# Spreading the cross-attention queries over the head masks on ScalarE instead of by small transfers

## The chip, the cores and the metric

One core of a Trainium2 chip runs the whole kernel. The metric is device time in microseconds (us), the median of repeated runs. The core has five engines that run side by side, each through its own instruction queue in program order: TensorE (matmuls, PE in the rows), VectorE (DVE), ScalarE (ACT), GpSimd (POOL) and SyncE (SP), which here only issues transfers. They are ordered against each other by semaphores that the kernel waits on by hand. Data is moved by 16 DMA engines.

## The reference, cut to what matters

A decoder layer on x of 32 x 128 x 128 with a context of the same shape: top-32 self-attention, then 16-head cross-attention, then a routed feed-forward layer with 8 experts. The change is in the cross-attention, whose heads have only 8 of the 128 features each:

```python
Q = (query @ Wq.T + bq).reshape(B, S, H, HD).transpose(0, 2, 1, 3)   # H = 16, HD = 8
K = (key @ Wk.T + bk).reshape(B, S, H, HD).transpose(0, 2, 1, 3)
V = (value @ Wv.T + bv).reshape(B, S, H, HD).transpose(0, 2, 1, 3)
scores = jnp.einsum('bhqd,bhkd->bhqk', Q, K) / jnp.sqrt(jnp.asarray(HD, Q.dtype))
weights = jax.nn.softmax(scores, axis=-1)
out = jnp.einsum('bhqk,bhkd->bhqd', weights, V)
```

## The kernel before, in words

The 32 batches are worked in 8 groups of 4 (g = 0 to 7). Cross-attention of group g is **pass** g. A pass has 8 **steps** (n = 0 to 7), two for each batch j. In the same pass the queues also carry the self-attention and the projections of groups g+2 and g+3 and the normalisation, routing and storing of group g-1. After pass 7 come 39 tiles of the feed-forward layer. The order of every queue is written out by hand in `run(g)` and `step(n, before, after)` of each engine; there is no scheduler.

Scores of 16 heads are made on TensorE in four **strips** of 32 partitions, each with four heads of 8 features. One strip's matmul has 32 x 128 weights and a moving operand of 32 x 512: the 128 tokens four times, once for each head of the strip, with all features of the other three heads zero. This "masked" copy is what the change is about. There are two such products. `s1` (L1565) takes natural queries and masked keys, and VectorE takes from its result the maximum per head and query (`head_max`, L1004, `neg_hmax`). `s2` (L1576) takes natural keys and masked queries. Into the same bank `s2_shift` (L1583) adds minus the maximum, and ScalarE's `exps` (L1309, `weights`) take the exponential. `pv` (L1607) multiplies by the values. The maxima reach `s2_shift` by `hmax_split` on VectorE (L1017, L1019), a transpose on TensorE (`hmax_rows`, L1593) and `hmax_out` on ScalarE (L1300, `hmax_t`).

Waits that matter below: `s2` waits until the exponentials of two strips before are done, as it overwrites their bank; `s1` waits for VectorE's maxima in the same way; the first two strips of a `pv` wait for `hmax_t` of the next batch. So each step has s2 x2, s1 x2, (hmax_rows), s2_shift x2 on TensorE, and (hmax_out), exps x2 on ScalarE.

The natural queries of group e = g+2 are projected at the end of pass g (step 7) and ScalarE copies them with their bias to `q_nat`, a part of the buffer `q_room` (`cross_queries`, L1302, semaphore `xq_ready`). The masked queries, `q_masked`, lie in `q_room` too, in a ring of two groups (`Q_RING`), each four blocks of 128 x 512. For group 0 ScalarE makes the four blocks itself, by a copy with a factor per partition, `head_mask`, that is one or zero (L1503). For groups 1 to 7 SyncE issues 16 transfers per group, 8 partitions x 2 KB each, that put the features of one head in their place in blocks that GpSimd had set to zero at the start (L919) or that have stayed zero since (L599, `mask_queries`, in pass g for group g+1). The keys are spread in the same way by 16 transfers per group, and this stays. `s2` of a group's first strip waits for all of `xq_masked`.

In the rows ScalarE's `xn<-x` is `normed_x1` (L1316 x4, step 5, group g+2), `xn_t`, scores and other self-attention buffers are pieces of `self_room`, and `ctx_t` also takes the transposed `xn2`.

Of the kernel before, what the change touches and what calls it, by code (L numbers as in the profile page):

```python
# [6 lines left out]
def preln_decoder_kernel(nc, T, out):  # L7
# [6 lines left out]
    ACT = mybir.ActivationFunctionType  # L14
# [5 lines left out]
    H, HD = 16, 8  # L20
    G = 4
# [24 lines left out]
    with ExitStack() as stack:  # L46
# [111 lines left out]
        def carve(which, n):  # L158
# [36 lines left out]
            attn_done x1_ready x1_bv_ready  # L195
            xn2_transposed xn2_t_ready xq_done xq_ready xq_masked first_masked mask_made early_step taken_step
            ctx_transposed ctx_t_ready xk_done xk_ready xk_masked xv_done xv_ready ones_made
            s1_done s1_max hmax_step hmax_split hmax_transposed hmax_t_ready s2_done s2_exp pv_done pvt_ready att_transposed
            wsum_inv_ready attended_ready x2_ready
            feats_transposed feats_t_ready aff_done aff_ready aff_max_ready aff_exp_ready aff_den_ready alpha_ready  # L200
            rstd2_step rstd2_ready base_ready pay_ready tokens_ready blank_made blanks_stored bv_made zeros_made q_zeros_made k_zeros_made wvo_done wvo_ready
            w1_loaded w1_rest_loaded b1_done b1_ready iota_made
# [77 lines left out]
        def later(g, first):  # L280

            return not isinstance(g, int) or g >= first
# [278 lines left out]
        def _(sp):  # L561
# [38 lines left out]

            def mask_queries(g):

                if not 1 <= g < NG:
                    return
                wait_alone(sp, s["xq_ready"], g + 1)
                if g == 1:
                    wait_alone(sp, s["q_zeros_made"], 1)
                if later(g, 2):
                    wait_alone(sp, s["xq_masked"], 16 * H * (g - 1))
                if later(g, Q_RING):  # L610
                    wait_alone(sp, s["s2_done"], 16 * (g - Q_RING + 1))
                spread_heads(q_masked, q_nat[:, (g % 3) * GS:(g % 3 + 1) * GS], (g % Q_RING) * MASKED, "xq_masked")

            def mask_keys(g):
# [14 lines left out]
            def run(g):  # L629
                if g >= 0:  # L630
                    load_later_x(g)
                    mask_queries(g + 1)
                if 0 < g + 3 < NG:
                    wait_alone(sp, s["ctx_transposed"], g + 3)
                    wait_alone(sp, s["ctx_loaded"], 16 * (g + 3))
                    load_ctx(g + 3)
                mask_keys(g + 2)
                if g < 0:
                    load_later_x(g)
                    mask_queries(g + 1)  # L640
                if isinstance(g, int) and g == NG - 3:
                    load_biases()
# [118 lines left out]
        def _(pool):  # L761
# [156 lines left out]

            pool.memset(q_masked[:, MASKED:2 * MASKED], 0.0).then_inc(s["q_zeros_made"], 1)  # L919
            norm_rstd(pool, 0, 0)  # L920
# [365 lines left out]
        def _(act):  # L1286
# [101 lines left out]
            def cross_queries(e):  # L1388
                if 0 <= e < NG:
                    if later(e, 3):  # L1390
                        act.wait_ge(s["s2_done"], 16 * (e - 2))
                    evacuate(q_nat[:, (e % 3) * GS:(e % 3 + 1) * GS], cross_bank[:, :], "xq_done", e + 1, "xq_ready", 2)

            def normed_x1(e):
                if 0 <= e < NG:
                    if later(e, 1):
                        act.wait_ge(s["xn2_transposed"], e)
                    norm(1, e, x1[:, :], xn2[:, :])
# [19 lines left out]
            def run(g):  # L1418
                has_f, has_c, has_e, has_s = stages(g)
                e, h = g + 2, g + 3  # L1420

                def step(n, before, after):

                    scores_first = isinstance(g, int) and g == 0 and n == 0
                    g1, j1 = following(g, n // 2, 1)
                    if not scores_first:
                        before()
                    if n % 2 == 1 and has_c and g1 < NG:
                        hmax_out(g1, j1)
                    if has_c:  # L1430
                        exps(g, n // 2, n % 2 * 2)
                        exps(g, n // 2, n % 2 * 2 + 1)
                    if scores_first:
                        before()
                    after()
                    batches = G * g + n // 2
                    if n % 2 == 0 and has_c and batches > 0:
                        evacuate(pvt[:, :], pvt_bank[:, 0:256], "pv_done", 4 * batches, "pvt_ready")
                    if g == NG - 1 and n == 7:
                        evacuate(pvt[:, :], pvt_bank[:, 0:256], "pv_done", 4 * B, "pvt_ready")  # L1440
# [59 lines left out]
            act.wait_ge(s["mask_made"], 2)  # L1500
            act.wait_ge(s["xq_ready"], 1)
            for m in range(G):
                act.activation(at(q_masked, m * GS, GS), q_nat[:, 0:GS], ACT.Copy, scale=head_mask[:, m:m + 1])\  # L1503
                   .then_inc(s["first_masked"], 1)
            probs_out(1)
# [7 lines left out]
        def _(pe):  # L1513
# [54 lines left out]
            def s2(g, j, u):  # L1568
                q = 16 * g + 4 * j + u
                if later(g, 1) or q >= 2:  # L1570
                    pe.wait_ge(s["s2_exp"], q - 1)
                if j == 0 and u == 0 and g == 0:
                    pe.wait_ge(s["first_masked"], G)
                if j == 0 and u == 0 and g > 0:
                    pe.wait_ge(s["xq_masked"], 16 * H * g)
                pe.matmul(s2_bank[:, (u % 2) * GS:(u % 2 + 1) * GS], natural(k_nat, g, j, u), masked(q_masked, Q_RING, g, j, u),  # L1576
# [334 lines left out]
```

## Time and profile before

| | |
|---|---|
| median of 3 runs | 411.51 us (410.72 to 412.42) |
| the profiled execution | 409.8 us, its span 408.1 us |
| span around the profile | 1.7 us |
| TensorE / VectorE / ScalarE / GpSimd busy | 87% / 73% / 59% / 48% of the span |
| pass 0 begins (first `s2`) | about 50 us |
| passes 1 to 4, each | about 31.3 us |
| mean granted TensorE clock | 0.949 of full |

A timeline row gives start and duration in us, the engine, the line of the kernel, the operation, the output and inputs, and how many instructions are merged (x2 counts two; an fp32 matmul shows as two). Behind it in brackets stands how long the engine was idle just before it and what ended that. Durations overlap: an engine takes up the next instruction before the record of the last one ends, so starts are the better ruler.

### The profile page before, as it was taken

What the parts mean: (1) busy time and instruction counts of PE and PEld (TensorE: products, weight loads), DVE (VectorE), ACT (ScalarE), POOL (GpSimd) and SP (SyncE); (2) the same over time, 40 slices, a digit from 0 to 9 for tenths busy, and PEclk for the clock granted to TensorE, in tenths of its full rate; (3) what the DMA queues carried; (4) which work ended last, traced back from release to release, by engine and by line L of the source; (5) the groups of instructions that cost most, each with busy time, mean ns of one, the idle gap of its engine ahead of it and who ended that gap; (6) DMA issues with size and microseconds to landing.
All of it is one profiled execution on the core that took longest, in us unless ns stands there. A gap on an engine that the chain in (4) does not pass through costs nothing.

```text
span 408.1 us, 11367 instructions
## 1 busy us (share of the span) xinstructions
PE 353.6 (87%) x3499; PEld 248.9 (61%) x3499; DVE 296.8 (73%) x1218; ACT 240.8 (59%) x527; POOL 195.7 (48%) x348
## 2 busy tenths in 40 slices
PE   5988989998999999999998899998696857899990
PEld 4766645545555655654654555555486747899980
DVE  6799846997898898897798858577653646566660
ACT  1464446666777777776766665656263445677750
POOL 4687400320650573574483375736576245344451
PEclk9799969999999999999999999999769698999996
DMA  5415201232121122221211122000322133433310
GB/s 136 155 23 174 55 13 25 51 103 49 31 77 29 46 84 54 51 82 51 51 45 36 24 88 52 24 35 28 86 74 83 50 125 120 112 92 92 87 50 0
DMA packets 30155, 26.96 MB, mean 66 GB/s; under 512 B 5891, under 2 KB 25479, under 8 KB 30096
## 3 DMA queue, kind: packets, MB, share of 16 engines
q1 hardware_dynamic: 26016, 19.59, 18.3%
q0 software_dynamic: 2784, 6.37, 4.6%
q8 instruction: 29, 0.48, 0.5%
q10 hardware_dynamic: 1296, 0.28, 0.5%
q14 instruction: 30, 0.25, 0.2%
HBM read 14.73 MB, written 8.01 MB: 56 GB/s over the span
## 4 chain that ended last, share of the span: by engine, by line
PE 50%; DVE 12%; issue 11%; ACT 9%; SPq 3%; POOL 2%; DVEq 2%; another core or an unknown queue 1%; DMA 1%; ACTq 0%; POOLq 0%
PE s_bank L1576 13%; PE pvt_bank L1607 5%; PE s_bank L1583 4%; PE s_bank L430 4%; DVE q_room L466 3%; PE cross_bank L1518 3%; ACT weights L1309 3%; PE cross_bank L1523 2%; ACT self_room L1300 2%; PE s_bank L1565 2%; ACT xn L1316 2%; PE cross_bank L1671 2%; PE cross_bank L1644 2%; PE att_bank L1729 2%; DVE x_in L481 2%
## 5 line engine op out<-in xcount | busy, mean ns | idle before, releaser
L1004 DVE TENSOR_REDUCE neg_hmax<-s_bank 128x4 f32<-128x512 f32 x128 | 82.4, 687 | 40.6 <-PE s_bank L1565 40.2
L1309 ACT ACTIVATE weights<-s_bank 128x512 f32<-128x512 f32 x128 | 69.8, 596 | 29.1 <-PE s_bank L1583 25.1
L1576 PE MATMUL s_bank<-q_room,k_room 32*128 32x512 f32 x256 | 78.9, 639 | 0.2
L1565 PE MATMUL s_bank<-k_room,q_room 32*128 32x512 f32 x256 | 76.9, 647 | 0.2 <-DVE neg_hmax L1004 0.2
L519 POOL DMA_INDIRECT out<-x_in,k_room x39 | 37.9, 972 | 48.1 <-DVE x_in L481 33.4
L805 POOL TENSOR_TENSOR x<-x_bv,attended 128x128 f32<-128x128 f32 x32 | 14.5, 453 | 76.4 <-DVE attended L1031 76.4
L466 DVE TENSOR_TENSOR q_room<-s_bank,b_cols 128x512 f32<-128x512 f32 x39 | 27.0, 692 | 30.4 <-PE s_bank L430 21.8
L1607 PE MATMUL pvt_bank<-weights,xv 128*32 128x128 f32 x1024 | 42.3, 283 | 3.3 <-ACT hmax_t L1300 3.1
L430 PE MATMUL s_bank<-k_room,self_room 128*128 128x128 f32 x312 | 44.7, 290 | 0.0
L501 ACT ACTIVATE self_room<-w,gamma_t 128x512 f32 x39 | 28.2, 722 | 23.5 <-PE s_bank L430 15.8
L430 PEld LDWEIGHTS s_bank<-k_room,self_room 128*128 128x128 f32 x312 | 41.3, 206 | 0.0
L816 POOL DMA_INDIRECT routed_rows<-pay,slot x32 | 33.0, 1030 | 12.1 <-issue 7.6
L1607 PEld LDWEIGHTS pvt_bank<-weights,xv 128*32 128x32 f32 x1024 | 25.1, 111 | 18.9 <-ACT weights L1309 9.1
L1576 PEld LDWEIGHTS s_bank<-q_room,k_room 32*128 32x128 f32 x256 | 24.9, 183 | 15.6 <-issue 8.2
L996 DVE MATCH_REPLACE8 self_room<-best,self_room 128x128 f32<-128x128 f32 x128 | 34.1, 284 | 0.0
L1583 PEld LDWEIGHTS s_bank<-hmax_t,head_sel 32*128 32x128 bf16 x512 | 20.3, 93 | 17.6 <-issue 14.4
L507 ACT ACTIVATE q_room<-q_room 128x512 f32<-128x512 f32 x39 | 24.6, 630 | 10.4 <-DVE q_room L466 5.3
L727 POOL TENSOR_SCALAR var_eps<-moments 128x4 f32<-128x4 f32 x24 | 4.9, 203 | 53.3 <-DVE moments L688 52.8
L1583 PE MATMUL s_bank<-hmax_t,head_sel 32*128 32x128 bf16 x512 | 29.9, 217 | 0.0
L444 PE MATMUL pvt_bank<-w,q_room 128*128 x160 | 23.7, 294 | 6.2 <-ACT q_room L507 6.2
L1300 ACT ACTIVATE hmax_t<-pvt_bank 128x128 bf16<-128x128 bf16 x32 | 8.9, 277 | 32.8 <-PE pvt_bank L1593 31.1
L990 DVE MAX8 best<-self_room 128x8 f32<-128x128 f32 x128 | 27.7, 282 | 0.0
(213 smaller groups left out, 739.0 us busy)
## 6 DMA issues: line engine op xcount, KB each, us to landing
k_room<-routed_rows SPq DMA_DIRECT2D x39, 130.0 KB
w<-in_w SPq DMA_DIRECT2D x16, 256.0 KB, 4.0
x_in<-in_x SPq DMA_DIRECT2D x8, 256.0 KB, 3.3
ctx_in<-in_ctx SPq DMA_DIRECT2D x8, 256.0 KB, 2.9
k_room<-k_room SPq DMA_DIRECT2D x128, 16.0 KB
q_room<-q_room SPq DMA_DIRECT2D x112, 16.0 KB
routed_rows<-blank SPq DMA_DIRECT2D x9, 130.0 KB
out<-x_in,k_room POOLq DMA_INDIRECT x39
```

The lines of the kernel that those rows point to most:

```text
L430: m = pe.matmul(s1_bank[:, (k % 2) * F + c * 128:(k % 2) * F + (c + 1) * 128], ffn_w1[k % 2][:, c * 128:(c + 1) * 128], ffn_row_t[k % 2], ...
L466: dve.tensor_tensor(by_chunk(ffn_hid[k % 2]), by_chunk(s1_bank[:, (k % 2) * F:(k % 2 + 1) * F]), spread(at(b1_cols, e * FC, FC).rearrange( ...
L501: act.activation(ffn_w1[k % 2], at(w1, e * F, F), ACT.Identity, scale=at(gamma_t, e, 1)).then_inc(s["w1_picked"], 1)
L519: pool.indirect_dma_start(out=out_rows, out_offset=bass.IndirectOffsetOnAxis(ap=ffn_row[k][:, TOKEN:TOKEN + 1].bitcast(U32), axis=0), in_= ...
L816: pool.indirect_dma_start(out=rows, out_offset=bass.IndirectOffsetOnAxis(ap=slot[:, at0:at0 + 1].bitcast(U32), axis=0), in_=pay[:, at0, :] ...
L996: dve.match_replace(at(left, b * S, S), best8[:, b, r, :], at(src, b * S, S), TAKEN)\
L1004: dve.tensor_reduce(neg_hmax[:, first:first + 4], bank.rearrange("p (h k) -> p h k", k=S), AX.X, ALU.max, negate=True).then_inc(s["s1_max" ...
L1309: act.activation(weights[:, u, :], s2_bank[:, (u % 2) * GS:(u % 2 + 1) * GS], ACT.Exp, scale=HEAD_SCALE).then_inc(s["s2_exp"], 1)
L1565: pe.matmul(s1_bank[:, (u % 2) * GS:(u % 2 + 1) * GS], natural(q_nat, g, j, strip(u)), masked(k_masked, K_RING, g, j, strip(u)), start=Tru ...
L1576: pe.matmul(s2_bank[:, (u % 2) * GS:(u % 2 + 1) * GS], natural(k_nat, g, j, u), masked(q_masked, Q_RING, g, j, u), start=True, stop=False)
L1583: m = pe.matmul(s2_bank[:, (u % 2) * GS + i * S:(u % 2) * GS + (i + 1) * S], head_sel[32 * u:32 * (u + 1), i, :], hmax_t[32 * u:32 * (u + ...
L1607: m = pe.matmul(pvt_bank[32 * i:32 * (i + 1), (u % 2) * S:(u % 2 + 1) * S], xv[:, block:block + 32], weights[:, u, i * S:(i + 1) * S], sta ...
```

## The change

`mask_queries` moves from SyncE to ScalarE. For groups 1 to 7 ScalarE makes the four masked blocks by the same operation as for group 0, one behind each of four steps of the pass before: steps 2, 4, 6 and 7 (in pass 0 steps 3, 4, 6 and 7). SyncE's 16 transfers per group and GpSimd's one setting to zero of 128 x 2048 go. `xq_masked` now counts four per group.

```diff
@@ SyncE @@
-            def mask_queries(g):
-
-                if not 1 <= g < NG:
-                    return
-                wait_alone(sp, s["xq_ready"], g + 1)
-                if g == 1:
-                    wait_alone(sp, s["q_zeros_made"], 1)
-                if later(g, 2):
-                    wait_alone(sp, s["xq_masked"], 16 * H * (g - 1))
-                if later(g, Q_RING):
-                    wait_alone(sp, s["s2_done"], 16 * (g - Q_RING + 1))
-                spread_heads(q_masked, q_nat[:, (g % 3) * GS:(g % 3 + 1) * GS], (g % Q_RING) * MASKED, "xq_masked")
@@ SyncE, run(g) @@
                 if g >= 0:
                     load_later_x(g)
-                    mask_queries(g + 1)
@@ GpSimd @@
-            pool.memset(q_masked[:, MASKED:2 * MASKED], 0.0).then_inc(s["q_zeros_made"], 1)
@@ ScalarE @@
+            def mask_queries(e, m):
+                if 0 <= e < NG:
+                    act.wait_ge(s["xq_ready"], e + 1)
+                    if later(e, Q_RING):
+                        act.wait_ge(s["s2_done"], 16 * (e - Q_RING + 1))
+                    at0 = (e % Q_RING) * MASKED + m * GS
+                    act.activation(at(q_masked, at0, GS), q_nat[:, (e % 3) * GS:(e % 3 + 1) * GS], ACT.Copy,
+                                   scale=head_mask[:, m:m + 1]).then_inc(s["xq_masked"], 1)
@@ ScalarE, run(g) @@
+                mask_steps = (3, 4, 6, 7) if g == 0 else (2, 4, 6, 7)
                     if n % 2 == 0 and has_c and batches > 0:
                         evacuate(pvt[:, :], pvt_bank[:, 0:256], "pv_done", 4 * batches, "pvt_ready")
+                    if n in mask_steps:
+                        mask_queries(g + 1, mask_steps.index(n))
@@ TensorE, s2 @@
-                if j == 0 and u == 0 and g == 0:
-                    pe.wait_ge(s["first_masked"], G)
-                if j == 0 and u == 0 and g > 0:
-                    pe.wait_ge(s["xq_masked"], 16 * H * g)
+                if j == 0 and u == 0:
+                    pe.wait_ge(s["xq_masked"], G * (g + 1))
```

How the queues stand at the places of which the prediction speaks. First ScalarE's queue in steps 4 and 5 of pass 1 (passes 0 to 5 have the same rows here, pass 0 without `feats_t`), before:

```order
L1309 ACTIVATE weights<-s_bank 128x512 x2
L1300 ACTIVATE feats_t<-cross_bank 128x512
L1300 ACTIVATE pvt<-pvt_bank 128x256
L1316 ACTIVATE xn<-x,mean_rstd,rstd 128x128 x4
L1300 ACTIVATE hmax_t<-pvt_bank 128x128
L1309 ACTIVATE weights<-s_bank 128x512 x2
```

and now (its lines stand 16 lower there):

```order
L1293 ACTIVATE weights<-s_bank 128x512 x2
L1284 ACTIVATE feats_t<-cross_bank 128x512
L1284 ACTIVATE pvt<-pvt_bank 128x256
L1384 ACTIVATE q_room<-q_room,head_mask 128x512
L1300 ACTIVATE xn<-x,mean_rstd,rstd 128x128 x4
L1284 ACTIVATE hmax_t<-pvt_bank 128x128
L1293 ACTIVATE weights<-s_bank 128x512 x2
```

One masking operation (L1384) has come between the copy of `pvt` and `normed_x1`, ahead of `hmax_out` and the exponentials of step 5.

Second ScalarE's queue from step 7 of pass 5 to step 1 of pass 6, where no group is left for `context`, before:

```order
L1309 ACTIVATE weights<-s_bank 128x512 x2
L1302 ACTIVATE q_room<-cross_bank,bias_cols 128x512
L1309 ACTIVATE weights<-s_bank 128x512 x2
L1300 ACTIVATE pvt<-pvt_bank 128x256
L1300 ACTIVATE hmax_t<-pvt_bank 128x128
```

and now:

```order
L1293 ACTIVATE weights<-s_bank 128x512 x2
L1286 ACTIVATE q_room<-cross_bank,bias_cols 128x512
L1384 ACTIVATE q_room<-q_room,head_mask 128x512
L1293 ACTIVATE weights<-s_bank 128x512 x2
L1284 ACTIVATE pvt<-pvt_bank 128x256
L1284 ACTIVATE hmax_t<-pvt_bank 128x128
```

The fourth masking operation of group 6 has come between the copy of group 7's natural queries and the first exponentials of pass 6. In passes 0 to 4 the same row is followed by `context`'s copy of `ctx_t`; at the end of pass 6 there is no copy of natural queries, and it stands right behind the exponentials.

Third SyncE's queue in passes 4 to 6, before:

```order
L599 DMA q_room<-q_room 8x512 x16
L567 DMA ctx_in<-in_ctx 128x4x128
L599 DMA k_room<-k_room 8x512 x16
L599 DMA q_room<-q_room 8x512 x16
L599 DMA k_room<-k_room 8x512 x16
L585 DMA x_in<-in_b 128x1024
L599 DMA q_room<-q_room 8x512 x16
```

and now:

```order
L567 DMA ctx_in<-in_ctx 128x4x128
L599 DMA k_room<-k_room 8x512 x32
L585 DMA x_in<-in_b 128x1024
```

The transfers of the queries are gone, and what stood behind them moves up.

## Rows read from the trace of the kernel before

**Rows 1.** the page's part 1: busy us (share) and instructions of each engine.

```profile
PE 353.6 (87%) x3499; PEld 248.9 (61%) x3499; DVE 296.8 (73%) x1218; ACT 240.8 (59%) x527; POOL 195.7 (48%) x348
```

**Rows 2.** pass 4: us; busy PE, PEld, DVE, ACT, POOL; PEclk; DMA share, GB/s.

```profile
183.30:215.10 31.80, 29.53 (x340) 17.77 (x339) 26.95 (x122) 21.31 (x49) 17.98 (x34) 1.00 0.18 48
```

**Rows 3.** the chain that ended last, in pass 4.

```profile
204.52 0.73 ACT xn L1316 x2
```

**Rows 4.** group 0's masking: ns min/median/max, first and last start; and its timeline.

```profile
L1503 ACT ACTIVATE q_room<-q_room,head_mask x4: 708/708/713, 41.6 to 43.5; 128x512 f32<-128x512 f32 x4
...
41.64 2.54 ACT L1503 ACTIVATE q_room<-q_room,head_mask 128x512 f32<-128x512 f32 x4
```

**Rows 5.** timeline of SyncE's queue, pass 1.

```profile
88.72 10.68 SPq L599 DMA_DIRECT2D q_room<-q_room  x16
```

**Rows 6.** ScalarE's exponentials in 89.4:99.4 and 112.5:119.3 (count, busy us, mean ns).

```profile
L1309 ACT ACTIVATE weights<-s_bank 128x512 f32<-128x512 f32 x4 | 2.2, 595 | 0.7 <-PE s_bank L1583 0.7
...
L1309 ACT ACTIVATE weights<-s_bank 128x512 f32<-128x512 f32 x5 | 2.8, 610 | 0.0
```

**Rows 7.** timeline of ScalarE, pass 4 and the start of pass 5.

```profile
197.96 0.28 ACT L1300 ACTIVATE hmax_t<-pvt_bank 128x128 bf16<-128x128 bf16 x1 [2.26 <-PE pvt_bank L1593]
...
204.38 1.65 ACT L1316 ACTIVATE xn<-x,mean_rstd,rstd 128x128 f32<-128x128 f32 x4
...
205.92 0.28 ACT L1300 ACTIVATE hmax_t<-pvt_bank 128x128 bf16<-128x128 bf16 x1
...
211.49 0.21 ACT L1409 ACTIVATE aff_exp<-aff_max 128x4 f32<-128x4 f32 x1 [0.52 <-DVE aff_max L1131]
...
212.15 0.28 ACT L1300 ACTIVATE hmax_t<-pvt_bank 128x128 bf16<-128x128 bf16 x1 [0.45 <-issue]
...
213.77 0.69 ACT L1302 ACTIVATE q_room<-cross_bank,bias_cols 128x512 f32<-128x512 f32 x1 [0.26 <-PE cross_bank L1523]
```

**Rows 8.** timeline of TensorE, pass 4 and the start of pass 5.

```profile
188.11 0.70 PE L1576 MATMUL s_bank<-q_room,k_room 32*128 32x512 f32 x2
...
189.19 0.23 PE L1593 MATMUL pvt_bank<-ident_bf,hmax_parts 128*128 128x128 bf16 x1
...
206.35 0.64 PE L1607 MATMUL pvt_bank<-weights,xv 128*32 128x128 f32 x16 [0.44 <-ACT hmax_t L1300]
...
210.46 0.70 PE L1576 MATMUL s_bank<-q_room,k_room 32*128 32x512 f32 x2
...
211.83 0.23 PE L1593 MATMUL pvt_bank<-ident_bf,hmax_parts 128*128 128x128 bf16 x1
...
215.11 0.70 PE L1576 MATMUL s_bank<-q_room,k_room 32*128 32x512 f32 x2
```

**Rows 9.** timeline of VectorE, pass 4.

```profile
202.48 1.29 DVE L1004 TENSOR_REDUCE neg_hmax<-s_bank 128x4 f32<-128x512 f32 x2 [1.17 <-PE s_bank L1565]
...
209.43 1.29 DVE L1004 TENSOR_REDUCE neg_hmax<-s_bank 128x4 f32<-128x512 f32 x2
```

**Rows 10.** timeline of TensorE, step 7 of pass 0.

```profile
83.83 1.26 PE L1576 MATMUL s_bank<-q_room,k_room 32*128 32x512 f32 x4
...
86.17 0.23 PE L1593 MATMUL pvt_bank<-ident_bf,hmax_parts 128*128 128x128 bf16 x1
```

**Rows 11.** ScalarE in passes 5 and 6.

```profile
234.54 1.65 ACT L1316 ACTIVATE xn<-x,mean_rstd,rstd 128x128 f32<-128x128 f32 x4 [0.77 <-POOL mean_rstd L743]
...
243.56 0.69 ACT L1302 ACTIVATE q_room<-cross_bank,bias_cols 128x512 f32<-128x512 f32 x1 [0.22 <-PE cross_bank L1523]
...
259.80 0.28 ACT L1300 ACTIVATE hmax_t<-pvt_bank 128x128 bf16<-128x128 bf16 x1 [0.88 <-PE pvt_bank L1593]
...
266.50 1.08 ACT L1309 ACTIVATE weights<-s_bank 128x512 f32<-128x512 f32 x2
```

**Rows 12.** TensorE: first `s2` of passes 6 and 7.

```profile
243.96 0.70 PE L1576 MATMUL s_bank<-q_room,k_room 32*128 32x512 f32 x2
...
267.32 1.00 PE L1576 MATMUL s_bank<-q_room,k_room 32*128 32x512 f32 x2
```

More of the change, by code:

```diff
@@ L195, in preln_decoder_kernel @@
             attn_done x1_ready x1_bv_ready
-            xn2_transposed xn2_t_ready xq_done xq_ready xq_masked first_masked mask_made early_step taken_step
+            xn2_transposed xn2_t_ready xq_done xq_ready xq_masked mask_made early_step taken_step
             ctx_transposed ctx_t_ready xk_done xk_ready xk_masked xv_done xv_ready ones_made
@@ L200, in preln_decoder_kernel @@
             feats_transposed feats_t_ready aff_done aff_ready aff_max_ready aff_exp_ready aff_den_ready alpha_ready
-            rstd2_step rstd2_ready base_ready pay_ready tokens_ready blank_made blanks_stored bv_made zeros_made q_zeros_made k_zeros_made wvo_done wvo_ready
+            rstd2_step rstd2_ready base_ready pay_ready tokens_ready blank_made blanks_stored bv_made zeros_made  k_zeros_made wvo_done wvo_ready
             w1_loaded w1_rest_loaded b1_done b1_ready iota_made
@@ L639, in run @@
                     load_later_x(g)
-                    mask_queries(g + 1)
                 if isinstance(g, int) and g == NG - 3:
@@ L1500, in _ @@
             act.wait_ge(s["mask_made"], 2)
-            act.wait_ge(s["xq_ready"], 1)
             for m in range(G):
-                act.activation(at(q_masked, m * GS, GS), q_nat[:, 0:GS], ACT.Copy, scale=head_mask[:, m:m + 1])\
-                   .then_inc(s["first_masked"], 1)
+                mask_queries(0, m)
             probs_out(1)
```

## The prediction

> **What bounds the kernel now.** I read the page's busy shares first: TensorE is busy for 87% of the span, VectorE 73%, ScalarE 59% [rows 1]. That says TensorE, but the shares are means over stages, so I took one pass. In pass 4 TensorE is busy for 29.53 of 31.80 us, VectorE for 26.95 and ScalarE for 21.31, with a granted clock of 1.00, the 2.4 GHz level [rows 2]. ScalarE thus has 10.5 us of room in a pass, and four operations more would fit as a sum. What counts is where they are put, since it works in order and TensorE waits for it at several places. The chain that ended last shows one: in each of passes 1 to 4 it leaves TensorE once for `normed_x1` (the row shown, four such) [rows 3]. ScalarE's timeline says why: `normed_x1` begins at 204.38 and `hmax_out` at 205.92, both without idle time before them [rows 7], and TensorE stands for 0.44 us until `pv` can start at 206.35, 0.15 after `hmax_out` ends at 206.20 [rows 8]. This is step 5, and ScalarE is the bound there. VectorE is the second clock: from 202.48 on it works without a gap through steps 5, 6 and 7 [rows 9].
>
> **What is removed, and what that is worth.** SyncE issues group 2's 16 transfers from 88.72 to 99.40 (10.68 us) [rows 5], while the `s2` that needs them comes with pass 2, about 31 us after 89. Nothing in the passes waits for them. The same holds for what SyncE has behind them: the context of group g+3 and the masked keys of group g+2 are used a pass later. GpSimd's setting to zero lies at the start, where it then waits for VectorE anyway. So I put the removed part at 0. The bounds: nothing below 0 from waits, since no wait goes; whether the traffic itself slows the engines is seen in ScalarE's exponentials, 595 ns each with these transfers in flight and 610 without [rows 6]. What keeps it at 0 is that all of it is covered by a whole pass of TensorE work.
>
> The Trainium skill bears on this from two sides (DMA: Bandwidth & Descriptors, Rules for kernel authors). It says that transfers under 64 KB are mostly overhead, and it also says that the fixed cost of a transfer is hidden when it is issued early and waited for late. These transfers are 16 KB, so the first would count 112 overheads as a gain, the second none; the sum by the second is the one above, and the trace agrees with it by the 10.68 us that end 20 us early [rows 5].
>
> **What one masking operation costs.** Group 0 has the very operation: 708 ns each, and four of them take 2.54 us, so one begins (2.54 - 0.71) / 3 = 0.61 us after the other [rows 4]. 28 of them are 17 us more on ScalarE. For each I ask what it stands in front of.
>
> *Step 2 (and step 3 in pass 0).* Before `hmax_out` ScalarE is idle for 2.26 us [rows 7]. Hidden: 0. Without this cover it would be 0.61 a pass.
>
> *Step 6.* `affinity_exp` waits 0.52 us for VectorE and the next `hmax_out` is idle for 0.45 more [rows 7], 0.97 together against 0.61. Hidden: 0. In pass 6 the least such gap at its steps 2, 4 and 6 is 0.88 us [rows 11]: 0.
>
> *Step 4, passes 1 to 4.* Here nothing is idle: `normed_x1` starts at once behind `pvt` [rows 7]. The operation moves `normed_x1`, `hmax_out` and the exponentials of step 5 by 0.61, and with them `pv` and the `s2` of step 6, where the matmuls wait in line. Behind it TensorE is in order, so the loss goes on until TensorE meets a wait on something that was not moved. There is one, in step 7: a step without such a wait has 1.08 us from `s2` to `hmax_rows` (188.11 to 189.19), step 7 has 1.37 (210.46 to 211.83) [rows 8]. The 0.29 more is the second `s1` waiting for VectorE's maxima, whose pair starts at 209.43 with no idle time before it [rows 9], and would still do so, since its `s1` results would come at about 209.0. So 0.29 is paid back: 0.61 - 0.29 = 0.32 a pass, 1.3 us for four. VectorE itself isn't late. The bounds: 0.61 if nothing is paid back, 0 if VectorE holds more.
>
> *Step 4, pass 0.* In step 7 of that pass the same distance is 86.17 - 83.83 = 2.34 us [rows 10], 1.26 more than 1.08, so a delay of 0.61 vanishes: 0.
>
> *Step 4, pass 5.* `normed_x1` is idle for 0.77 us waiting for GpSimd [rows 11], more than 0.61: 0.
>
> *Step 7, into passes 1 to 5.* The fourth block comes behind the copy of the new natural queries, which starts at 213.77 [rows 7]. The masking starts some 0.57 later (the pitch of that copy, estimated as its 0.69 less the usual overlap of 0.12), ends 0.71 after that, and TensorE needs 0.15 (as with `pv` above): 213.77 + 0.57 + 0.71 + 0.15 = 215.20, while `s2` of pass 5 now starts at 215.11 [rows 8]. So 0.09 late; passes 1 to 4 begin in the same way. Five times: 0.4 us. It is so small because TensorE first has `pv` and four transposes of the context. Bounds: 0 and 0.3 each, if a weight load waits too.
>
> *Step 7 of pass 5, into pass 6.* No group is left whose context would be transposed, so the cover is gone. The copy starts at 243.56 [rows 11], the block is ready for TensorE at 243.56 + 1.43 = 244.99, and `s2` now starts at 243.96 [rows 12]: **1.03 us late**. Queued behind it on TensorE are both `s1` and `s2_shift`, for which VectorE's maxima and ScalarE's exponentials wait; all move along.
>
> *Step 7 of pass 6, into pass 7.* There is no copy, and the block comes behind two exponentials that start at 266.50 and take 1.08 together [rows 11]. With the usual overlap it starts at 267.47, ends at 268.18, and `s2` can go at 268.33 instead of 267.32 [rows 12]: **1.01 us late**. Bounds of these two: 0.9 and 1.2 each.
>
> **Sum.** 1.3 + 0.4 + 1.0 + 1.0 = 3.7 us. The profiled execution took 409.8, so it would take 413.5. That execution is 1.7 under the median of the runs, 411.5, to which the same 3.7 is added: **415.2 us**, 0.9% slower. With all lower bounds the sum is 0 + 0 + 1.8 = 1.8, with all upper ones 5 x 0.61 + 5 x 0.3 + 2.4 = 7.0.
>
> **The rivals.**
> (a) *Nothing is paid back at step 7*, because VectorE's work moves with TensorE's: 5 x 0.61 + 0.4 + 2.0 = 5.5, so 417.0. For it: the maxima do read what TensorE writes. Against it: VectorE has no gap there.
> (b) *More is paid back*: VectorE is busy for 26.95 of 31.80 us [rows 2], and if its order holds the passes, the 0.32 and the 0.09 vanish and perhaps part of the steps into 6 and 7. That is 2.0 or less, 413.5 or less, no difference that can be told (a measurement of this kernel tells about 0.5%, 2 us, from no change). Against it: VectorE waits for TensorE in each pass (1.17 us in pass 4 [rows 9]).
> (c) *The transfers cost something now*, so that the kernel gets faster. They are in flight for 7 x 10.7 = 75 us. To end even they must slow what lies beside them by 3.7 / 75 = 5%, and for 2 us of gain by 8%; at 10% it would be 7.5 - 3.7, so 407.7. Against it: 595 ns with and 610 ns without them [rows 6], no sign of even 1% in this direction. The Trainium skill (SBUF — State Buffer, SBUF: two separate sides) says that engines and DMA use different ports and cannot contend, by which this rival gains 0; the trace agrees.
> (d) *More is lost*: gaps that just suffice (0.97 in step 6, 0.77 in pass 5) do not, at 0.3 us for five passes each, on top of (a): 419 or more.
>
> **Chances.** The forecast 0.60, (a) 0.15, (b) 0.15, (c) 0.05, (d) 0.05. Slower by over 0.5% are the forecast, (a) and (d): 0.80. Within 0.5%: 0.15. Faster: 0.05. The range leaves out (c), (d) and the lower half of (b): 412.9 to 418.2.
>
> **What would show it.** In the profile after: about 28 masking operations more of 0.71 us on ScalarE and 112 transfers fewer. In passes 1 to 4 the idle time of TensorE before `pv` in step 5 grows from 0.44 to about 1.05, and `s2` to `hmax_rows` in step 7 shrinks from 1.37 to 1.08; each of these passes is 0.4 longer. The first `s2` of passes 6 and 7 stands behind ScalarE's masking, each by 1 us. Pass 0 is unchanged. I would be wrong if `pv` waits no longer in step 5, if the first `s2` of pass 6 is held by something else, or if the feed-forward tiles, which the change doesn't touch, take a different time.

## The result, and the profile of the changed kernel

| | before | changed |
|---|---|---|
| median of 4 runs each | 411.12 us (408.89 to 412.42) | 416.98 us (415.88 to 422.52) |
| ratio, 95% interval | | 1.0155 (1.0099 to 1.0212) |
| profiled execution | 409.8 us, span 408.1 | 415.88 us, span 414.1 |
| mean granted TensorE clock | 0.949 | 0.938 |

The ratio says about 1.5% slower; the medians differ by 5.9 us, where 3.7 us had been forecast. Each ratio here and below leaves out the runs more than 1.5% above the fastest of their kernel, and since a fall of TensorE's clock makes just such a run, the experiments give the mean of all runs beside it.

The page of the kernel before, the queue of the hardware transfers (packets, MB, share), and the groups of `s2` (L1576) and `pv` (L1607), out<-in xcount | busy, mean ns | idle before, releaser:

```profile
q1 hardware_dynamic: 26016, 19.59, 18.3%
...
L1576 PE MATMUL s_bank<-q_room,k_room 32*128 32x512 f32 x256 | 78.9, 639 | 0.2
...
L1607 PE MATMUL pvt_bank<-weights,xv 128*32 128x128 f32 x1024 | 42.3, 283 | 3.3 <-ACT hmax_t L1300 3.1
```

The page of the changed kernel, with the busy shares, and `s2` at L1569, `pv` at L1600:

```profile
PE 357.1 (86%) x3499; PEld 250.9 (61%) x3499; DVE 297.4 (72%) x1218; ACT 257.1 (62%) x555; POOL 194.2 (47%) x347
...
q1 hardware_dynamic: 24224, 17.76, 15.7%
...
L1569 PE MATMUL s_bank<-q_room,k_room 32*128 32x512 f32 x256 | 79.5, 653 | 2.2 <-ACT q_room L1384 1.9
...
L1600 PE MATMUL pvt_bank<-weights,xv 128*32 128x128 f32 x1024 | 43.2, 286 | 6.6 <-ACT hmax_t L1284 6.5
```

ScalarE has 28 instructions and 16.3 us more than in [rows 1], GpSimd has one instruction fewer, and 1792 packets of 1 KB are gone, the 112 transfers of 16 KB. The two groups name the two places where TensorE now stands: `s2` for the masked queries (1.9 us, nothing before) and `pv` for `hmax_t` (6.5 us, 3.1 before).

Groups of the changed kernel, the masking alone (duration ns min/median/max; first and last start), and who waited for it:

```profile
L1384 ACT ACTIVATE q_room<-q_room,head_mask x32: 707/712/759, 41.2 to 269.6; 128x512 f32<-128x512 f32 x32
...
who waited for it (us, times):
  PE s_bank L1569: 1.9, 2
```

(The 32 are the 28 new ones and group 0's four.) Of the 28 new operations the profile names a direct waiter for only two. Pass 4 on ScalarE's timeline, to be read against [rows 7]:

```profile
204.53 0.40 ACT L1284 ACTIVATE pvt<-pvt_bank 128x256 f32<-128x256 f32 x1
204.79 0.74 ACT L1384 ACTIVATE q_room<-q_room,head_mask 128x512 f32<-128x512 f32 x1
205.41 1.65 ACT L1300 ACTIVATE xn<-x,mean_rstd,rstd 128x128 f32<-128x128 f32 x4
206.94 0.28 ACT L1284 ACTIVATE hmax_t<-pvt_bank 128x128 bf16<-128x128 bf16 x1
...
212.23 0.71 ACT L1384 ACTIVATE q_room<-q_room,head_mask 128x512 f32<-128x512 f32 x1
...
214.29 0.28 ACT L1284 ACTIVATE hmax_t<-pvt_bank 128x128 bf16<-128x128 bf16 x1 [1.25 <-PE s_bank L1576]
...
215.42 0.70 ACT L1286 ACTIVATE q_room<-cross_bank,bias_cols 128x512 f32<-128x512 f32 x1
215.99 0.74 ACT L1384 ACTIVATE q_room<-q_room,head_mask 128x512 f32<-128x512 f32 x1
```

The step-4 operation has pushed `xn` 0.62 us back with nothing idle around it (204.79 to 205.41). The step-6 operation (212.23) delays nobody in the usual case, but the 1.25 us of idle time behind it here is no usual case: in passes 1 to 3 of this profile the same `hmax_out` waits 0.18 us, and so it does in pass 4 of another profile of the same kernel (experiment 9):

```profile
210.52 0.28 ACT L1284 ACTIVATE hmax_t<-pvt_bank 128x128 bf16<-128x128 bf16 x1 [0.18 <-PE pvt_bank L1586]
```

So the gap there, 0.97 in two parts before [rows 7], just suffices, with 0.18 left. The 1.25 us hold up everything behind them; experiment 4's profile has the like in its pass 4 (1.27 us), outside falls of the clock no other profile has it, and what held ScalarE is not shown. The step-7 operation follows the copy by 0.57 us. TensorE's timeline of the changed kernel, the answer to [rows 8] and [rows 12]:

```profile
207.37 0.64 PE L1600 MATMUL pvt_bank<-weights,xv 128*32 128x128 f32 x16 [1.05 <-ACT hmax_t L1284]
...
211.48 0.70 PE L1569 MATMUL s_bank<-q_room,k_room 32*128 32x512 f32 x2
...
212.55 0.23 PE L1586 MATMUL pvt_bank<-ident_bf,hmax_parts 128*128 128x128 bf16 x1
...
216.87 0.70 PE L1569 MATMUL s_bank<-q_room,k_room 32*128 32x512 f32 x2
...
246.28 0.70 PE L1569 MATMUL s_bank<-q_room,k_room 32*128 32x512 f32 x2 [0.96 <-ACT q_room L1384]
...
268.93 0.65 PE L1600 MATMUL pvt_bank<-weights,xv 128*32 128x128 f32 x16 [0.59 <-ACT hmax_t L1284]
270.51 1.13 PE L1569 MATMUL s_bank<-q_room,k_room 32*128 32x512 f32 x2 [0.94 <-ACT q_room L1384]
```

The idle time before `pv` is 1.05 instead of 0.44, and in step 7 `s2` to `hmax_rows` is 212.55 - 211.48 = 1.07 instead of 1.37: 0.61 lost and 0.30 paid back. The first `s2` of passes 6 and 7 stands for 0.96 and 0.94 us. But the last row holds something else: that pair of matmuls takes 1.13 us, where the one before took 0.70. The windows around it (us; busy PE, PEld, DVE, ACT, POOL; PEclk; DMA share, GB/s) say why:

```profile
268.00:270.00 2.00, 0.99 (x18) 0.51 (x18) 1.59 (x4) 1.49 (x4) 1.10 (x2) 1.00 0.18 67
270.00:272.00 2.00, 1.49 (x8) 0.61 (x9) 0.15 (x1) 0.37 (x1) 1.48 (x2) 0.66 0.00 0
272.00:274.00 2.00, 2.00 (x29) 1.16 (x24) 1.41 (x3) 1.08 (x2) 0.00 (x0) 0.50 0.18 67
274.00:276.00 2.00, 2.00 (x23) 0.90 (x25) 1.83 (x10) 0.96 (x3) 0.00 (x0) 0.99 0.00 0
```

Behind two idle stretches (0.59 and 0.94 us) the granted clock falls from 1.00 to 0.50, from the 2.4 to the 1.2 GHz level, for some 3 us. The profile before has 1.00 in the same 8 us of its own time. So the wait comes with a second bill, and that is what the experiments had to size.

**The ruler.** `hmax_rows` comes once for each batch and waits for the same things in every kernel, so its start tells how far a profile is behind the one before. For each step I take how that lag grows. In the changed kernel it grows by 0.33, 0.33, 0.33 and 0.31 from step 5 to step 7 of passes 1 to 4, by 0.08, 0.09 and 0.17 into passes 1 to 3, by -0.38 and 0.55 into passes 4 and 5, by 1.02 into pass 6, by 1.77 into pass 7, and by 4.4 from step 1 of pass 0 to step 5 of pass 7. The kernel of experiment 2, which has no new waits, has -0.39 and -0.45 into passes 4 and 5, so the profile before is long there by itself, and the 0.55 is 1.0 more than without waits: 0.1 for the step-7 operation and 0.9 for the hold of 1.25 us above (0.9 in experiment 4 too).

### The profile page after: what moved, and what is told of

It reads as the page before. It is cut to its first block, busy times and chain, and to the rows that moved or that the text cites. A ratio compares the mean times of both kernels' runs of the same rounds, so it can differ in the third digit from the quotient of the medians.

```text
span 414.1 us, 11299 instructions
## 1 busy us (share of the span) xinstructions
PE 357.1 (86%) x3499; PEld 250.9 (61%) x3499; DVE 297.4 (72%) x1218; ACT 257.1 (62%) x555; POOL 194.2 (47%) x347
## 4 chain that ended last, share of the span: by engine, by line
PE 49%; DVE 13%; ACT 11%; issue 10%; SPq 3%; DVEq 2%; POOL 1%; another core or an unknown queue 1%; DMA 1%; ACTq 0%; POOLq 0%
PE s_bank L1569 13%; PE pvt_bank L1600 5%; PE s_bank L1576 4%; PE s_bank L430 4%; DVE q_room L466 3%; PE cross_bank L1513 3%; ACT weights L1293 3%; ACT xn L1300 3%; PE cross_bank L1518 2%; ACT self_room L1284 2%; PE self_bank L444 2%; DVE x_in L481 2%; DVE neg_hmax L988 2%; PE cross_bank L1664 2%; PE cross_bank L1637 2%
## 5 line engine op out<-in xcount | busy, mean ns | idle before, releaser
L1569 PE MATMUL s_bank<-q_room,k_room 32*128 32x512 f32 x256 | 79.5, 653 | 2.2 <-ACT q_room L1384 1.9
L1560 PE MATMUL s_bank<-k_room,q_room 32*128 32x512 f32 x256 | 75.8, 654 | 0.2 <-DVE neg_hmax L988 0.2
L1600 PE MATMUL pvt_bank<-weights,xv 128*32 128x128 f32 x1024 | 43.2, 286 | 6.6 <-ACT hmax_t L1284 6.5
L430 PEld LDWEIGHTS s_bank<-k_room,self_room 128*128 128x128 f32 x312 | 42.2, 210 | 0.0
L1600 PEld LDWEIGHTS pvt_bank<-weights,xv 128*32 128x32 f32 x1024 | 25.4, 112 | 22.6 <-issue 12.6
L1569 PEld LDWEIGHTS s_bank<-q_room,k_room 32*128 32x128 f32 x256 | 24.8, 186 | 17.4 <-issue 9.8
L1576 PEld LDWEIGHTS s_bank<-hmax_t,head_sel 32*128 32x128 bf16 x512 | 20.7, 94 | 19.2 <-issue 16.1
L1576 PE MATMUL s_bank<-hmax_t,head_sel 32*128 32x128 bf16 x512 | 30.1, 220 | 0.0
L444 PE MATMUL pvt_bank<-w,q_room 128*128 x160 | 24.7, 303 | 4.2 <-ACT q_room L507 4.2
L717 POOL TENSOR_TENSOR rstd<-var_eps,minus_half 128x4 f32<-128x4 f32 x24 | 24.6, 1024 | 3.4 <-POOL var_eps L712 0.2
```

What stands on the lines that cost most here:

```text
L430: m = pe.matmul(s1_bank[:, (k % 2) * F + c * 128:(k % 2) * F + (c + 1) * 128], ffn_w1[k % 2][:, c * 128:(c + 1) * 128], ffn_row_t[k % 2], ...
L444: m = pe.matmul(bank[:, 0:D], ffn_relu[k % 2][:, c * 128:(c + 1) * 128], at(w2, e * (FC * D) + c * D, D), start=c == 0, stop=c == FC - 1)
L1560: pe.matmul(s1_bank[:, (u % 2) * GS:(u % 2 + 1) * GS], natural(q_nat, g, j, strip(u)), masked(k_masked, K_RING, g, j, strip(u)), start=Tru ...
L1576: m = pe.matmul(s2_bank[:, (u % 2) * GS + i * S:(u % 2) * GS + (i + 1) * S], head_sel[32 * u:32 * (u + 1), i, :], hmax_t[32 * u:32 * (u + ...
L1600: m = pe.matmul(pvt_bank[32 * i:32 * (i + 1), (u % 2) * S:(u % 2 + 1) * S], xv[:, block:block + 32], weights[:, u, i * S:(i + 1) * S], sta ...
```

## The experiments

Each was timed beside the kernel before on the same chip. Experiments 1 to 4 ran on one chip (before: median 409.82, mean 410.4, highest 416.3 us in 26 runs); the others on a second, on which everything is about 14 us shorter (before: 395.23 and 395.54, means 396.2 and 396.4, highest 402.0 us in 63 runs).

**1. The changed kernel again**, as a base:

> The changed kernel once more, as the yardstick for the others of this chip. My account of its 6 us: 3.7 us of waits by placement (step 4 in passes 1 to 4, step 7), and the rest from TensorE's clock, which in the profile of the changed kernel is at its lower level (0.50) from 270.7 to 274.7 us, right after TensorE stood 0.94 us for the last masking operation, and again when the feed-forward tiles start. By it: 1.010 to 1.018 of the kernel before. If the clock's part was chance of one execution, the median ratio is nearer 1.009.

Measured: 1.0148 (1.0096 to 1.0199), as expected; mean 7.2 us over before, single runs 413.3 to 421.5.

**2. Masking where ScalarE is idle.**

```diff
-                mask_steps = (3, 4, 6, 7) if g == 0 else (2, 4, 6, 7)
+                mask_steps = (2, 2, 3, 6) if g == 0 else (1, 2, 5, 6) if g == NG - 2 else (1, 2, 2, 5)
-                    if n in mask_steps:
-                        mask_queries(g + 1, mask_steps.index(n))
+                    for m in range(G):
+                        if mask_steps[m] == n:
+                            mask_queries(g + 1, m)
```

> All 28 masking operations stay on ScalarE, but each stands where ScalarE was idle: behind steps 1, 2, 2 and 5 (pass 0: 2, 2, 3, 6; pass 6: 1, 2, 5, 6). Theory of placement: no wait is left, so the time is that of the kernel before, 0.997 to 1.003. Rival, ScalarE's load itself costs (17 us more work on it, wherever it stands): as the changed kernel, 1.012 or more. Rival, the transfers cost something before: faster, 0.99 or less.

Measured: 0.997 (0.9942 to 0.9998), mean 1.2 us under before. The same 28 operations, 17 us of ScalarE, the same transfers gone, and the whole loss is gone with the places. In the timeline of this kernel, pass 4, `pv` waits as before:

```profile
204.74 0.64 PE L1601 MATMUL pvt_bank<-weights,xv 128*32 128x128 f32 x16 [0.44 <-ACT hmax_t L1284]
```

**3. Only the step-4 operations moved away** (`mask_steps` (2, 2, 6, 7), and (2, 5, 6, 7) from pass 1 on):

> Only the operation of step 4 moves, to step 5 (steps 2, 5, 6, 7; pass 0: 2, 2, 6, 7); the one of step 7 stays. Theory of placement: 1.3 us of the loss goes (0.32 in each of passes 1 to 4), the waits before the first product of passes 6 and 7 stay with 2.0 us and what the clock adds: 1.006 to 1.014, and in the profile the distance from s2 to hmax_rows in step 7 of passes 1 to 4 is 1.37 us again. Rival, nothing is paid back by VectorE's wait: 2.5 us or more below the changed kernel.

Measured: 1.0071 (1.004 to 1.0102), mean 2.5 us over before. The lag grows by 1.02 into pass 6 and by 1.87 into pass 7, where the clock fell again. In step 7 of passes 1 to 4 `s2` to `hmax_rows` is 1.35 to 1.38 us again, as expected. But by the ratios this kernel lies 3.2 us below experiment 1, where the theory gave 1.3 and the rival (nothing paid back) 2.5 or more. The ruler decides against that rival, with 0.31 to 0.33 lost in each of those passes of the changed kernel; experiment 1's profile has two long falls of the clock, in passes 2 and 4, this one has none, and that is where the rest fits.

**4. Only the step-7 operations moved away** ((2, 3, 4, 6), then (2, 2, 4, 6)):

> Only the operation of step 7 moves, to step 2 (steps 2, 2, 4, 6; pass 0: 2, 3, 4, 6); the one of step 4 stays. Theory of placement: the waits before the first products of passes 6 and 7 go, and with them the low clock behind them; 1.3 us stays from step 4: 1.001 to 1.006. If the clock's loss has nothing to do with those waits, it stays: 1.006 or more. Rival, nothing is paid back at step 7 of passes 1 to 4: 3.1 us stays, 1.007.

Measured: 1.0053 (1.0014 to 1.0091), but the mean is 4.8 us over before, and single runs lie from 408.4 to 421.6. The ratio is as expected, but the account behind it was not: I had tied the low clock to the step-7 waits, and it did not go with them. Its profile shows what makes the difference. TensorE's timeline in pass 1, then the windows behind it:

```profile
109.52 0.44 PE L1617 MATMUL att_bank<-ident,pvt 128*128 128x128 f32 x2
111.01 0.65 PE L1601 MATMUL pvt_bank<-weights,xv 128*32 128x128 f32 x16 [1.05 <-ACT hmax_t L1284]
111.58 1.22 PE L1570 MATMUL s_bank<-q_room,k_room 32*128 32x512 f32 x2
```

```profile
110.00:112.00 2.00, 0.99 (x20) 0.81 (x21) 1.97 (x7) 2.00 (x6) 1.83 (x4) 1.00 0.00 0
112.00:114.00 2.00, 2.00 (x16) 0.93 (x14) 1.85 (x12) 1.55 (x5) 2.00 (x3) 0.56 0.03 8
114.00:116.00 2.00, 2.00 (x11) 1.99 (x11) 1.43 (x4) 1.49 (x3) 1.36 (x3) 0.50 0.00 0
...
120.00:122.00 2.00, 2.00 (x12) 0.98 (x8) 1.88 (x7) 1.34 (x3) 0.24 (x1) 0.50 0.00 0
122.00:124.00 2.00, 1.69 (x21) 0.80 (x20) 1.55 (x12) 0.69 (x1) 0.21 (x1) 0.88 0.00 0
```

The engine stood for 1.05 us, as in all four of these passes; here, and in pass 3, the clock then fell to 0.50 for 10 us. In passes 2 and 4 the same wait left it at 1.00. In experiment 1's profile it fell in passes 2 and 4.

**5. The transfers alone.**

```diff
-                spread_heads(q_masked, q_nat[:, (g % 3) * GS:(g % 3 + 1) * GS], (g % Q_RING) * MASKED, "xq_masked")
...
-                    pe.wait_ge(s["xq_masked"], 16 * H * g)
+                    pe.wait_ge(s["q_zeros_made"], 1)
```

> The kernel before without the 112 transfers of the masked queries, and with nothing in their place: s2 of groups 1 to 7 reads masked queries that nobody has filled, so the scores of groups 1 to 7 are not those of the reference; every other instruction is there. It measures the removed part alone. My theory puts the removed part at 0: ratio 0.997 to 1.003. The rival that the transfers slow the engines beside them expects faster by 1% or more (0.99 or less); if 0.98, the change really gains 2% on this side and its ScalarE work costs over 3%. The experiment with masking in idle places gave 0.997 with the transfers gone and the 17 us of masking present, so up to 0.3% may appear here too.

Measured: 1.0006 (0.9972 to 1.004), mean 0.3 us under before. 112 covered transfers cost nothing.

**6. The waits filled.** The changed kernel with small matmuls put where TensorE stood. This tells whether the clock's falls come from TensorE standing still. Results of the added matmuls are never read.

```diff
+                    if n == 0 and g >= NG - 2:
+                        for _ in range(4):
+                            pe.matmul(self_bank[:, 0:128], ident[:, :], ident[:, :], start=True, stop=True)
                     if has_c:
                         s2(g, j, u)
...
+                    if n == 5 and g <= 4:
+                        pe.wait_ge(s["v_ready"], g + 4)
+                        for _ in range(4):
+                            pe.matmul(self_bank[:, 0:128], ident[:, :], ident[:, :], start=True, stop=True)
```

> The changed kernel, masking at the same steps, and in addition four matmuls of the identity (128 columns, fp32, about 0.85 us of work at 2.4 GHz, results never read) on TensorE where the new waits are: in step 5 of passes 0 to 4 ahead of pv, and ahead of the first s2 of passes 6 and 7. TensorE then works where it stood, while every instruction that matters waits as long as before. Theory (the granted clock falls behind the longer idle stretches, and this is what is paid beyond the 3.7 us of waits): the profile shows a granted clock of 1.00 through passes 1 to 5, and the ratio goes from 1.015 to 1.006 to 1.010 with runs close together. Rival (the clock falls for another reason, or the waits cost more than 3.7 by themselves): ratio stays at 1.015 or above and the runs spread over 413 to 421 us as before.

Measured: 1.0111 (1.0065 to 1.0158), a little above what I expected, in six runs whose mean is 3.9 us over before. The changed kernel had run on the other chip only, so both follow on one chip in 9 and 10.

**7. Experiment 3 with its waits filled** (the first of the two insertions above):

> The version in which only the step-4 operations are moved away (1.0071), and in addition the same four matmuls of the identity ahead of the first s2 of passes 6 and 7, where TensorE stands 0.94 us. Theory: the waits there stay (2.0 us, with 0.4 for passes 1 to 5), but the fall of the clock to 0.50 behind the step into pass 7 goes, which was worth 0.8 us: ratio 1.004 to 1.006. Rival (the clock's fall is not due to this wait): 1.007 or more, and the windows behind the first s2 of pass 7 still show 0.5 to 0.7.

Measured: 1.0048 (1.0021 to 1.0075), as expected, but the interval reaches that of experiment 3 and the mean is 3.2 us over before, so the ratio doesn't decide. Its profile held 1.00 from 268 to 275 us, behind the place that was filled, and had fallen to 0.50 in pass 5, at a place that the change doesn't touch (below).

**8. The idle places again:**

> The masking in idle places once more (steps 2, 2, 3, 6 of pass 0, 1, 2, 5, 6 of pass 6, 1, 2, 2, 5 of the others): it gave 0.997 [0.994, 1.000]. If that is a gain, it comes again with its interval under 1; if it is no change, 0.998 to 1.002. No theory here explains a gain of more than 0.3%.

Measured: 0.999 (0.9959 to 1.0021), mean 0.8 us over before. So 0.997 was no gain that holds: no version here beats the kernel before.

**9 and 10. Changed and filled on one chip:**

> The changed kernel once more, so that the filled version below has it on the same chip: 1.0148 before. Theory: 3.7 us of waits (1.009) and on top the falls of the granted clock to 0.50 behind them, some executions with and some without: 1.012 to 1.018 over the runs kept, single runs up to 8 us over the lowest.

> The version with four matmuls of the identity where TensorE stood (1.011 before, with an interval from 1.006 to 1.016; its profiled execution held a granted clock of 1.00 through passes 1 to 5 and was 3.6 us behind the profile of the kernel without transfers at the end of pass 7, which is the 3.7 of waits). Theory: lower than the changed kernel of this call by 0.3 to 0.7%, so 1.008 to 1.011. Rival (the clock is not what is paid beyond the waits): the same ratio as the changed kernel within 0.2%.

Measured: changed 1.0087 (1.0038 to 1.0136), filled 1.0086 (1.0044 to 1.0128). By these ratios the rival would be right, and my expectation for both was missed. But five of the twelve changed runs are not in the ratio, and these are 403.5 to 409.9 us, above every one of 63 runs of before. Over all runs the changed kernel is 5.4 us over before by the mean and 6.0 by the median, the filled one 2.7 and 3.1, and its highest run is 402.1. So by what the ratio keeps, both cost the waits alone, and what the filling changes lies in the runs left out of it: the mean falls by 2.7 us (two standard errors, worked out from the runs, 2.7). The profiles agree that it takes away falls. In TensorE's timeline the filling lies in the gap (`pv` begins 1.22 us after the filling began, the last 0.16 idle) and the lag grows there as without it; only ahead of passes 6 and 7 does it cost about 0.1 us. The clock of the filled kernel stays at 1.00 from 60 to 275 us:

```profile
109.86 1.06 PE L1781 MATMUL self_bank<-ident 128*128 128x128 f32 x8
111.08 0.65 PE L1600 MATMUL pvt_bank<-weights,xv 128*32 128x128 f32 x16 [0.16 <-ACT hmax_t L1284]
```

```profile
60.00:275.00 215.00, 203.60 (x2397) 123.19 (x2389) 175.76 (x751) 160.56 (x360) 98.19 (x199) 1.00 0.15 43
```

**11 and 12. The same pair for the step-4 operation alone:**

> The version in which only the step-4 operations are left in their place (1.0053, twelve runs from 408 to 422): waits of 1.3 us. Theory: the lowest runs at 1.000 to 1.003, and others higher by steps of about 3.6 us for each fall of the clock behind the 1.05 us of idle time in step 5; ratio 1.003 to 1.010.

> The same with the four matmuls of the identity in step 5 of passes 0 to 4, ahead of pv. Theory: the waits stay (1.3 us) and the steps of 3.6 us go: ratio 1.002 to 1.005, highest run no higher above the lowest than in the kernel before. Rival: the same ratio and spread as the unfilled one of this call.

Measured: unfilled 0.9995 (0.9928 to 1.0062), with only four runs of twelve in the ratio; filled 1.0074 (1.0038 to 1.011). Over all runs the unfilled version is 6.1 us over before by the mean, with runs up to 413.1; the filled one 1.7, up to 402.2. Both ratios miss what I expected, the filled one by being too high: it stands for 2.9 us, where the waits are 1.3 and the mean of all runs says 1.7. The ratio makes most of this difference itself: it leaves out 11 of 34 runs of before, which lowers their mean by about 1.5 us, and one of twelve of the filled kernel, which lowers it by 0.4. Between the means of all runs the filling gains 4.4 us (two standard errors 3.5). The spread came out as expected.

The profile of the unfilled one has a fall at a place that is not the change's: in pass 5 `pv` has an idle time of 0.83 us, which the kernel before has too (0.82). The row and its windows:

```profile
234.87 0.64 PE L1601 MATMUL pvt_bank<-weights,xv 128*32 128x128 f32 x16 [0.83 <-ACT hmax_t L1284]
```

```profile
230.00:232.00 2.00, 1.73 (x29) 1.15 (x27) 2.00 (x9) 2.00 (x5) 0.94 (x2) 1.00 0.53 195
232.00:240.00 8.00, 7.17 (x62) 4.72 (x56) 4.54 (x10) 5.21 (x12) 6.22 (x17) 0.76 0.11 37
240.00:246.00 6.00, 6.00 (x40) 2.77 (x39) 2.63 (x8) 2.45 (x6) 5.10 (x7) 0.50 0.13 46
```

It also gives the price of one fall. Three `hmax_rows` of this profile, and the same three of the filled one, whose clock did not fall:

```profile
233.11 0.23 PE L1587 MATMUL pvt_bank<-ident_bf,hmax_parts 128*128 128x128 bf16 x1
...
243.44 0.29 PE L1587 MATMUL pvt_bank<-ident_bf,hmax_parts 128*128 128x128 bf16 x1
...
250.63 0.23 PE L1587 MATMUL pvt_bank<-ident_bf,hmax_parts 128*128 128x128 bf16 x1
```

```profile
234.65 0.23 PE L1587 MATMUL pvt_bank<-ident_bf,hmax_parts 128*128 128x128 bf16 x1
...
241.58 0.23 PE L1587 MATMUL pvt_bank<-ident_bf,hmax_parts 128*128 128x128 bf16 x1
...
247.47 0.23 PE L1587 MATMUL pvt_bank<-ident_bf,hmax_parts 128*128 128x128 bf16 x1
```

17.52 us against 12.82: 4.7 us for one fall. My expectations had said 3.6, since I had read only the first of the two distances (10.33 against 6.93, 3.4, and in pass 1 the 0.33 of the wait beside it); 1.3 comes in the next. Taken over the same two distances, against a profile of the same placement whose clock held, the other five long falls cost 4.6 to 4.8 us as well.

All profiles of kernels with new waits together. The lag's growth is that from step 1 of pass 0 to step 5 of pass 7, less that of a kernel without new waits on the same chip (-0.6 for idle places on the first; -1.9, the mean of experiments 5 and 8, on the second). Falls are those between 60 and 275 us; one at the start of pass 0, within 51 to 60 us, is in seven of all fourteen profiles, the one of before among them, and lies ahead of the ruler's start:

```
kernel                         waits forecast   lag grown   falls in the profile
   changed, first profile           3.7            4.9      short one, pass 7
3  step 4 moved     (chip 1)        2.4            3.2      short one, pass 7
4  step 7 moved     (chip 1)        1.3           11.5      passes 1 and 3
1  changed          (chip 1)        3.7           12.1      passes 2 and 4
7  3, filled        (chip 2)        2.4            6.8      pass 5
11 step 7 moved     (chip 2)        1.3            6.1      pass 5
12 11, filled       (chip 2)        1.3            1.4      none
9  changed          (chip 2)        3.7            3.3      none
6  filled           (chip 2)        3.7            3.5      none
10 filled           (chip 2)        3.7            3.6      none
```

(The chip of the first profile isn't known; it is reckoned with the first, whose times it has.) Where no fall is in the profile, the lag is what was forecast, within 0.4. Where there are long falls, the rest is 4.7 for each, within 0.5, experiment 4's with the 0.9 of its hold in pass 4 in it. With the short one it is 0.8, and 1.2 in the first profile, which has such a hold too.

## Why the prediction was right, and what it left out

**What is removed: 0.** Right. Without the transfers the kernel before takes 1.0006 of its time, and rival (c) falls. Experiment 5 agrees with the Trainium skill's rule (DMA: Bandwidth & Descriptors, Rules for kernel authors) that an early issue and a late wait hide a transfer's fixed cost.

**The price of an operation and steps 2, 3, 6.** Right: 0.71 us, and nobody waits for these. Moved together into such places, all 28 cost nothing (0.997 and 0.999). Rival (d) falls too: the gap behind step 6 sufficed, but with only 0.18 us left, and the 0.77 of pass 5 sufficed as well (the lag grows by 0.01 there).

**Step 4 in passes 1 to 4: 0.32 each.** Right, measured 0.31 to 0.33, by the very two distances named. Rivals (a) and (b) fall here: of 0.61 about 0.3 was paid back, neither less nor more. That the median, 416.98, is rival (a)'s 417.0 is chance, since its mechanism is not in the trace. Pass 0 and pass 5: 0, as said.

**Step 7: 0.09, then 1.03 and 1.01.** 0.08 or 0.09 into each of passes 1 to 5, experiment 9's lag less experiment 5's. In these five the profile names nobody who waits for the block, so that `s2` is late for it rests on the sum, which fits. Into pass 6 1.02. Into pass 7 1.01 was too much where the clock held: in experiment 9 the lag grows by 0.1 there, 0.7 more than without the new waits, and by 0.7 in experiment 1's profile too. So in this one step part of rival (b) was right. With the clock's fall it was 1.77 in the first profile.

**What the sum lacked: the clock.** The measured 416.98 lies in the stated range of 412.9 to 418.2, and in profiles whose clock held the waits come to 3.3 to 3.6, where the forecast rests on 3.7. But the kernel lost 5.9 us by the first medians, and by the means of all runs 7.2, 7.2 and 5.4; with the waits filled 3.9 and 2.7. The range was drawn for more or less of the waits. That it covers the clock's part too is luck: 7.2 us over the 411.5 that the forecast starts from would be 418.7, outside it. The prediction read a granted clock of 1.00 in pass 4 [rows 2] and took it as given, though its own steps made TensorE stand for 1.05 us instead of 0.44 four times. The missing term, as the runs give it: 4 falls behind 20 such waits (passes 1 to 4 of the five profiles that have them unfilled), 0 behind 12 filled ones, and 0 in the 24 passes 1 to 4 of the six profiles without. That is 4 x 4/20 x 4.7 = 3.8 us in the mean. The step into pass 7 cost 0.8 more than forecast with its short fall (1.77 or 1.87 against 1.01) and 0.3 less without, each in two of four profiles, so 0.25 in the mean. Together 3.7 + 3.8 + 0.25 = 7.7, against 7.2, 7.2 and 5.4 measured. This is an estimate and no more: the four falls lie in two of the five profiles, and at one in five, twelve waits without a fall would come by chance once in fifteen times. What carries the claim is these counts together with the means and spreads of the two filled pairs.

The Trainium skill tells of a kernel with a like loss (TensorE: Matmul & The Clock Gate, A second HAM failure mode: psum-queue depth-cycling): there brief idling between groups of matmuls, frequent enough, lets the clock swing between its two levels, and throughput is lost between the bursts. The windows of experiment 4 agree as far as the swing goes, with 0.50 for 10 us behind 1.05 us of idle time; the stretch comes only once in a pass here. It would have been a rival of the prediction, at 4.7 us a fall by these runs.

**The rest of the profiled span.** Of its 6.0 us, 4.4 came in the passes and 0.5 was gained ahead of them. The remaining 2.1 lie in the feed-forward part, which the change doesn't touch, and for which the prediction had said that another time would prove it wrong. It does not: behind the last `hmax_rows` the changed kernel's first profile and the four of experiments 1 to 4 have 127.0 to 127.5 us, at a mean granted clock of 0.84 to 0.87, the kernel with idle places among them, whose runs are no slower than before. The one profile of before has 125.1 us at 0.89. So this belongs to that profile, and not to the change; why its clock was higher there is not shown.

## What to carry to other kernels

Idle time of an engine is no room as a sum: the same four operations per group cost nothing in idle places and 1.5% in places where another engine waits for what stands behind them, so read the idle time place by place, for the last group too, where the work that gave cover is missing. Where a change lengthens a wait of TensorE, add a term for its clock, with a chance and not as a fixed sum, and expect the runs to spread. When a ratio and its runs disagree, look at which runs the ratio leaves out.

## What the runs showed of the hardware

- The granted clock fell from 1.00 to 0.50 behind idle stretches of only 0.83 to 1.05 us in otherwise busy stretches (TensorE 129.5 of 140 us busy in experiment 9's passes), for some 3 to 10 us, and not each time: 4 of 20 behind 1.05 us, 2 of 14 behind the 0.83 us of pass 5, which every kernel here has. The length alone doesn't decide: a wait of 1.22 us for VectorE some 11 us earlier, in every one of these profiles, had no such fall behind it. One long fall costs 4.6 to 4.8 us of the span, in all six that were profiled.
- Four small matmuls in the gap, 1.06 us of work, were followed by no fall at any filled place of four profiles, and took the highest run from 413.1 to 402.2 and from 409.9 to 402.1.
- Two chips differ by 14 us of 410 with the same kernel. In the profiles of three kernels that ran on both (experiments 1 and 9, 2 and 8, 4 and 11) 12.7 to 15.0 us of it lie behind the last `hmax_rows`, in the feed-forward part, where the mean granted clock is 0.84 to 0.87 on one chip and 0.91 to 0.94 on the other.
